# First mixture's combining and the attention behind it, as two stages and as one by groups of four tiles

## The reference, cut to what matters

```python
# mixture (the end of it): top 2 of 8 experts, dense path abel_out
gate = sigmoid(concat([abel_out, moe_out]) @ gc_w + gc_b)
mixed = abel_out * (1.0 - gate) + moe_out * gate
x = x + (residual + mixed)
# causal attention, one head of 256 channels
Q = x @ Wq.T + bq ; K = x @ Wk.T + bk ; V = x @ Wv.T + bv
scores = where(causal, einsum('btc,bsc->bts', Q, K) * scale, -inf)
w = softmax(scores)
out = einsum('bts,bsc->btc', w, V) @ Wo.T + bo
```

## Time and profile before

| | |
|---|---|
| median of 3 runs | 1505.36 us (1504.7 to 1508.71) |
| the profiled execution, its own time | 1508.83 us |
| its span in the profile | 1507.2 us |
| PE matmuls busy | 1173.9 us (78%) |
| PE weight loads busy | 1014.6 us (67%) |
| DVE busy | 805.3 us (53%) |
| ACT busy | 574.3 us (38%) |
| POOL busy | 412.2 us (27%) |

### The profile page before, as it was taken

How to read it: one execution, slowest core, us unless ns; L and a number is a source line. 1 busy time by engine, 2 the same in 40 slices (tenths; PEclk the granted TensorE clock), 3 DMA queues, 4 the chain that set the end, 5 groups by cost and what they waited for, 6 DMA issues and landing times. The chain is left out here.

```text
span 1507.2 us, 25573 instructions
## 1 busy us (share of the span) xinstructions
PE 1173.9 (78%) x7238; PEld 1014.6 (67%) x7239; DVE 805.3 (53%) x2591; ACT 574.3 (38%) x1143; POOL 412.2 (27%) x478
## 2 busy tenths in 40 slices
PE   5896887853899999910899968998863599999940
PEld 5764665742688888810779857897752488888830
DVE  6445755746345445458544464444855344544538
ACT  1112552321454555544333323332432255455545
POOL 3002101656344444400000010000576244443410
PEclk9898995866899999965899988999776799999975
DMA  9300341436543333352000000000256573333346
GB/s 294 114 0 1 146 148 57 158 137 220 198 150 107 98 100 103 95 200 68 0 1 1 1 1 1 1 1 1 113 199 220 174 247 100 101 125 98 105 166 224
DMA packets 75431, 161.10 MB, mean 107 GB/s; under 512 B 11270, under 2 KB 36562, under 8 KB 75354
## 3 DMA queue, kind: packets, MB, share of 16 engines
q1 hardware_dynamic: 54794, 104.93, 20.2%
q0 software_dynamic: 19776, 54.45, 11.5%
q10 hardware_dynamic: 784, 0.79, 0.2%
HBM read 88.66 MB, written 71.47 MB: 106 GB/s over the span
## 5 line engine op out<-in xcount | busy, mean ns | idle before, releaser
L1426 PE MATMUL bank<-ew,rows 128*128 x852 | 308.4, 362 | 4.1 <-DVE rows L1076 2.8
L1427 PE MATMUL bank<-low_in,rows 128*128 x852 | 272.7, 320 | 0.0
L1428 PE MATMUL bank<-ew,rows 128*128 x852 | 272.7, 320 | 0.0
L1217 POOL DMA_INDIRECT results<-xh x142 | 141.9, 1000 | 310.6 <-DVE xh L1096 296.0
L1426 PEld LDWEIGHTS bank<-ew,rows 128*128 128x128 f32 x852 | 163.0, 191 | 16.4 <-issue 8.9
L1428 PEld LDWEIGHTS bank<-ew,rows 128*128 128x128 f32 x852 | 161.3, 189 | 11.9
L1427 PEld LDWEIGHTS bank<-low_in,rows 128*128 128x128 f32 x852 | 162.5, 191 | 6.9
L600 POOL TENSOR_TENSOR work<-work,mhalf 128x8 f32<-128x8 f32 (+1 forms) x20 | 37.9, 1897 | 460.7 <-DVE work L593 460.0
L1105 DVE TENSOR_TENSOR rows<-bank,rows 128x512 fp32r<-128x512 f32 x142 | 98.3, 692 | 98.4 <-ACT rows L164 98.4
L1076 DVE SCALAR_TENSOR_TENSOR rows<-bank,rows 128x256 fp32r<-128x256 f32 x142 | 60.3, 425 | 164.9 <-ACT rows L169 139.0
L1198 POOL DMA_INDIRECT slots_in<-xh,work x128 | 125.9, 984 | 67.7 <-issue 35.6
(11 more groups left out here) (295 smaller groups left out, 2002.1 us busy)
## 6 DMA issues: line engine op xcount, KB each, us to landing
xh<-slots_in POOLq DMA_DIRECT2D x142, 129.0 KB
xh<-results SPq DMA_DIRECT2D x16, 1032.0 KB, 6.2
low_in<-low SPq DMA_DIRECT2D x32, 512.0 KB
residual<-xs SPq DMA_DIRECT2D x16, 512.0 KB
dense<-ab SPq DMA_DIRECT2D x16, 512.0 KB
xs<-residual SPq DMA_DIRECT2D x16, 512.0 KB
ab<-dense SPq DMA_DIRECT2D x16, 512.0 KB
xs<-in_L_attn_a_x_dram SPq DMA_DIRECT2D x4, 1024.0 KB
```

The lines of the kernel that those rows point to most:

```text
L1217: pool.indirect_dma_start(out=yg, out_offset=bass.IndirectOffsetOnAxis(ap=back[j % RING], axis=0), in_=yr[j % RING], in_offset=None).then_ ...
L1426: pe.matmul(o, hi, f32r(high(c)), start=(c == 0), stop=False)
L1427: pe.matmul(o, hi, f32r(low(c)), start=False, stop=False)
L1428: last = pe.matmul(o, lo, f32r(high(c)), start=False, stop=(stop and c == chunks[-1]))
```

## The change

`mixture(0)` now ends when its results lie in memory; combining, for the first mixture alone, is part of `attention`. There, 32 rows n run in one sequence over both batches, and between them:

- SyncE fetches results and dense part of every group, three groups ahead at first; the fetching back of the dense part during the first mixture's experts is gone (`RETURNED`).
- VectorE combines group g + 2 during the rows of group g: `gate_in` after the first row's work, `gate_out` and half of `gather` after the second, the other half after the third, statistics after the fourth. `gather` is three multiply-adds per tile straight onto `xs`; ScalarE no longer scales anything for it. Groups 0 and 1 are combined before the first row.
- The keys, queries and values of group g + 1 are prepared within the rows of group g, in half parts (one bank each, banks 7 and 3): keys in the second row, values in the third, queries in the fourth. For the group that opens the second batch (SWITCH, 4) the keys are turned in row 15, and queries and values made at row 16, since bank 3 is in use by the scores before.
- Only one group of queries is kept. The outputs of two successive rows share bank 6, so that bank 7 is free. The split parts of `wa` and `wvo` have their own places and are made once, not once per batch. `prob` moves from `work` to the place of `xh`; there is one `ln` buffer, not two.

Its core (waits of the new helper functions as they stand; those like ones shown are left out):

```diff
-                    for g in range(NG + 2):
+                    for g in range(NG + 2) if r == 1 else ():
...
-                        for o, i in ((xs, xs_out), (ab, ab_out)):
+                        for o, i in RETURNED:
...
+                    for g in range(NG):
+                        k = place(g)
+                        if g >= 3:
+                            sp.wait_ge(x2_ok, 3 * GT * (1 if g == 3 else g))
+                        sp.dma_start(y_at[k].rearrange("p t k c -> p t (k c)"), y[:, tiles(g), :]).then_inc(y_ld[k], 16)
+                        sp.dma_start(ab_at[k].rearrange("p t c -> p (t c)"), ab_out[g]).then_inc(y_ld[k], 16)
...
+                    def gate_in(g):
+
+                        y = y_at[place(g)]
+                        v.wait_ge(y_ld[place(g)], 32 * (uses(g) + 1 if place(g) == 0 else 1))
+                        small(v.tensor_tensor(zz, y[:, :, :, C], wts[:, tiles(g), :], ALU.mult))
+                        settled()
+                        small(v.tensor_reduce(z, zz, AX.X, ALU.add))
+                        settled()
+                        small(v.scalar_tensor_tensor(z, z, gcb[:], zab[:, tiles(g)], ALU.add, ALU.add))
+                        settled()
+                        v.tensor_scalar(z, z, -87.0, None, ALU.max).then_inc(z_ok, 1)
...
+                    def gather(g, half):
+
+                        y, a = y_at[place(g)], ab_at[place(g)]
+                        some = range(half * GT // 2, (half + 1) * GT // 2)
+                        done = 3 * (GT * g + half * GT // 2)
+                        for k in range(3):
+                            for m, t in enumerate(some):
+                                if k >= 1:
+                                    v.wait_ge(x2_ok, done + (k - 1) * len(some) + m + 1)
+                                o = xs[:, g * GT + t, :]
+                                src, part = ((a[:, t, :], shut[:, t:t + 1]), (y[:, t, 0, 0:C], gw2[:, t, 0:1]),
+                                             (y[:, t, 1, 0:C], gw2[:, t, 1:2]))[k]
+                                v.scalar_tensor_tensor(o, src, part, o, ALU.mult, ALU.add).then_inc(x2_ok, 1)
...
+                    def key_part(g, c):
+                        pe.wait_ge(ln_ok, GT * (g + 1))
+                        after(pe, q_ok, KC * g)
+                        after(pe, v_ok, 2 * g)
+                        if g == SWITCH:
+                            pe.wait_ge(klow_ok, KC * g + c)
+                        for t in range(GT):
+                            last = pe.transpose(bank[:, key_bank(g, c), t * P:(t + 1) * P], ln[:, t, c * P:(c + 1) * P], ident[:])
+                        last.then_inc(lnT_ps, 1)
...
+                    def query_part(g, j):
+                        pe.wait_ge(klow_ok, KC * (g + 1))
+                        pe.wait_ge(wlow_ok, 2)
+                        if g == SWITCH:
+                            pe.wait_ge(exp_ok, BT * g // GB)
+                        elif g >= 1:
+                            pe.wait_ge(v_ok, 2 * (g + 1))
+                        for c in range(KC):
+                            last = split(bank[:, query_bank(g, j), :], lambda x: weight(WA, x, c, slice(j * P, (j + 1) * P)),
+                                         lambda y: keys[:, g % GB, y, c, :], c == 0, c == KC - 1)
+                        last.then_inc(q_ps, 1)
...
+                    def value_part(g, h):
+                        pe.wait_ge(klow_ok, KC * (g + 1))
+                        pe.wait_ge(wlow_ok, 2)
+                        if g == SWITCH or g == 0:
+                            pe.wait_ge(q_ok, KC * (g + 1))
+                        for t in range(h * GT // 2, (h + 1) * GT // 2):
+                            o = bank[:, value_bank(g, h), (t % 2) * C:(t % 2 + 1) * C]
+                            for c in range(KC):
+                                split(o, lambda x: keys[:, g % GB, x, c, t * P:(t + 1) * P],
+                                      lambda y: weight(WVO, y, c, slice(0, C)), c == 0, False)
+                            last = pe.matmul(o, onesb[0:2 * QROW + 1, :], vbp[:], start=False, stop=True, skip_group_check=True)
+                        last.then_inc(v_ps, 1)
+
...
+                    gather(1, 0)
+                    gather(1, 1)
+                    statistics(1)
+                    for n in range(NR + 1):
+                        g, q = ahead(n)
+                        if n >= 1:
+                            low_shares(n - 1, slice(0, 2))
...
+                            if g and q == 1:
+                                low_keys(g, 0)
+                            if g and q == 2:
+                                low_values(g, 0)
+                            highest(n)
+                            if g and q == 1:
+                                low_keys(g, 1)
+                            if g and q == 2:
+                                low_values(g, 1)
+                            if g and q == 3:
+                                for j in range(KC):
+                                    low_queries(g, j)
...
+                                low_shares(n - 1, slice(2, None))
+                                finish(n - 1)
...
+                        now = n // GT
+                        if n < NR and n % GT == 0 and now + 1 < NG:
+                            normalise(now + 1)
+                        if n < NR and now + 2 < NG:
+                            if n % GT == 0:
+                                gate_in(now + 2)
+                            if n % GT == 1:
+                                gate_out(now + 2)
+                                gather(now + 2, 0)
+                            if n % GT == 2:
+                                gather(now + 2, 1)
+                            if n % GT == 3:
+                                statistics(now + 2)
...
+                        if n >= 1:
+                            pe.wait_ge(exp_ok, n)
+                            for c in range(min(2, (n - 1) % BT // GT + 1)):
+                                turn(n - 1, c)
+                        if switching(n):
+                            for j in range(KC):
+                                query_part(SWITCH, j)
+                            weigh_row(n - 1)
+                            scores(n)
+                            for h in range(2):
+                                value_part(SWITCH, h)
```

431 lines of the change are left out of this document (269 added, 162 removed).

## The result

The changed kernel took **1456.14 us** (median of 4 runs, 1455.16 to 1460.08), the kernel before on the same chip 1505.03 (4 runs, 1501.61 to 1508.71). The ratio is 0.9676, with a 95% interval of 0.9659 to 0.9693: 48.9 us less, where the text said 39.7 less and 1466. The profiled execution took 1455.16, near its median, while that of before took 1508.83 and lay 3.8 above its own. So the two profiles differ by 53.7 us, 4.8 more than the medians.

The account below looks back on a forecast made before the run. TensorE bounds the rows and VectorE combining, with about 97 us of TensorE idle to win. 699 + 106.9 + 30.5 + 20 + 123.2 + 32.5 = 1012.1 for 1051.8, 39.7 us less: 1466, range 1448 to 1492.

Parts of the forecast that it names:

- The start: From fetching the results to the first row maximum: it comes at 699 us instead of 754.4.
- The lengths of the groups: Times between maxima: rows 0-3 25.2 us, 4-7 32.1, 8-11 43.6, row 15 to 16 20.
- The reason for rows 0 to 3 and 16 to 19: VectorE, with 20.3 us of work for 13.6 before in rows 0 to 3, sets the pace: +12 there.
- it all hides: Rival: added work hides, rows 0 to 3 take TensorE's 16.6 us, rows 4 to 7 30; 1441 to 1450, chance 0.06.
- VectorE over 80% busy: Sign in the new profile: VectorE over 80% busy from the first maximum at 699 to the fifth at about 724.
- Combining at the price of rows: Between rows: combining and preparation together give VectorE 14.7 us per group, lengthening rows 0 to 3 by 12.
- TensorE's added work in full: Groups 1 to 3 and 5 to 7: 7.2 us each of added TensorE work, charged at its whole duration.
- The normalising: Rows 8 to 11: 1.5 us for transposes that wait for the normalising, within 43.6 for 34.6.
- VectorE's order at 1 to 2 us more per row: Rival: VectorE's strict order costs sixteen rows with both works 16 to 32 us more; 1482 to 1498, chance 0.14.
- Low clock between rows: Rival: pauses in rows 0 to 7 and 16 to 23 keep TensorE at 1.2 GHz, 72 us more; 1538, chance 0.10.
- First fetches sharing the DMA engines: Rival: before the first row, first fetches share engines instead of coming in turn, 7 us later; 1473, no separate chance.
- Behind attention: The second mixture, 455 us of the same instructions, was left unchanged in the sum.

Follow-up runs that it names:

- e5: Changed kernel with all eight groups combined before the first row and only preparation left between rows: 1465.77 us, ratio to before 0.9953.
- e6: Changed kernel with two of three multiply-adds per tile cut to 8 of 256 columns in groups 2 to 7: 1424.60 us, ratio to before 0.9672.
- e9: Changed kernel with the values' 28 matmuls issued twice for groups 1 to 3 and 5 to 7: 1443.37 us, ratio to before 0.9805.
- e2: Changed kernel with the next group's normalising moved up behind the maximum of the group's first row: 1416.48 us, ratio to before 0.9621.
- e1: The changed kernel run again without edits, as yardstick on the experiments' chip: 1423.93 us against 1472.58 before, ratio 0.9669.
- e4: Changed kernel with ScalarE's exponential ahead of second-half key and value copies and queries' copies in short rows: 1426.95 us, ratio to before 0.9689.
- e3: Changed kernel with group 1's combining moved into VectorE's waits for group 0's queries and values: 1416.84 us, ratio to before 0.9617.
- e10: Changed kernel with the edits of e2 and e3 plus statistics of group 1 and later groups made earlier: 1411.43 us, ratio to before 0.9584.
- e11: Changed kernel with the edits of e2 and e3 plus 24 unread filler matmuls in the first rows: 1408.56 us, ratio to before 0.9564.
- e12: Changed kernel with the edits of e2 and e3, early statistics and filler matmuls all together: 1410.28 us, ratio to before 0.9582.

## Why the prediction was right or wrong, point by point

**The start** was right. First maximum at 699, measured 696.86, of which 2.1 us are the experts' earlier end. Every part came within about 2 us of its forecast: gate to transposes, queries, values (at the high clock, 684.80 on, where I took a middle one), the twelve sums in 4.83 for 4.9. From ask to use the fetches took 7.2 us, where the sum had 5.4 and 1.3 for the dense part, so 0.5 more, and the ask came 1.7 earlier than the sum's 655.5. That they come in turn and not shared held: a first group's wait of 7 us more did not occur.

**The lengths of the groups** were right to 1.1 us, except for rows 16 to 19 (28.5 forecast, 25.4 measured): 25.2, 32.1, 43.6, 36.2 and 20 against 24.1, 31.1, 42.9, 35.2 and 19.2. With the start these errors make up the 11.7 us by which attention ended ahead of 1012.1. The largest is that of rows 16 to 19: the values of group 4 behind row 16 and the warm start together were charged 3.3 us over rows 0 to 3, and 1.3 was measured. All errors have the same sign; what made the small ones was not tried.

**The reason for rows 0 to 3 and 16 to 19 was wrong.** The step "VectorE has 5.6 + 14.7 = 20.3 us for 13.6 before, so it sets the pace", with some 4 us of idle time (24.0) and 1.2 of clock, gave 25.2. By the same step rows without combining take 17 to 19, as the expectation of e5 says, and e5 measured 24.14. What is there instead is TensorE: the 16.6 us at the high clock that the prediction itself names under the rival "it all hides", 2.3 more for the low clock (18.86 busy), and 5.2 of waits, for transposes' input and for exponentials. Three of the 5.2 us lie in one chain, in the timeline of the changed kernel:

```profile
698.70 0.16 DVE L1666 SCALAR_TENSOR_TENSOR work<-work 128x4 f32<-128x4 f32 x1 [1.56 <-POOL work L606]
698.90 1.38 DVE L1670 TENSOR_SCALAR work<-xs,work 128x256 f32<-128x256 f32 x4
...
700.33 1.12 PE L1879 MATMUL bank<-ident,work 128*128 128x128 f32 x4 [2.17 <-DVE work L1670]
```

The root on GpSimd (1.6 us), then the normalising, then the transposes, with TensorE idle from the maximum to 700.33 but for one transpose. That the length came out right was luck: the sum by VectorE and the sum by TensorE happened to come out alike, and a forecast that hits a length says nothing of its cause. The prediction named "VectorE over 80% busy" as what would be seen; it was at 78%, close to that, and in e5 at 55% for the same length. A busy share was no test of this step, only a change of the load is.

**Combining at the price of rows** was the second consequence of that step. The 11.6 and 15 us for rows 0 to 3 and 16 to 19 were booked to both works together; the runs give all of it to the preparation and its waits, none to combining (e5, e6).

**TensorE's added work in full** was right. The prediction charged all 7.2 us per group although weight loads fill only 26.5 of 31.1 and 37.7 of 42.9 us. e9 is the test: 28 more matmuls lengthen each group by 3.2 to 3.4 us, as much as they are busy. The Trainium skill (Perfetto Trace Analysis, Identifying the Most-Contended Engine) judges TensorE's headroom by the share of peak arithmetic and by the busy share of weight loads. By the second of these there was room for these matmuls in the groups of 31 and 43 us; here the trace disagrees, since none was absorbed with weight loads at 85 to 88%. Busy matmuls were the measure of what one more would cost.

**The normalising** in rows 8 to 11 ("1.5 for transposes that wait") was right: 1.1 measured, and e2 takes it back.

**The rivals.** VectorE's order at 1 to 2 us more per row: no, and e6 shows that its load is not what counts. All hidden, 1441 to 1450: the measured 1456 lies nearer to it than its chance of 0.06 suggests, since combining does hide in full; what kept the time above is TensorE's waits and clock, not the amount of VectorE's work. Low clock between rows, 1538: no. The granted clock stays at 1.00 from 704 on with TensorE waiting once or twice per row. The section on depth-cycling that the prediction cited from the Trainium skill (TensorE: Matmul & The Clock Gate) has such short idling swing the clock; from the rise in the first rows to row 15 it did in no profile here, and behind row 16 it fell in five profiles (e1, e4, e5, e6, e9) and did not in two with the same order there (the changed kernel's first, e3), for 1.3 us. First fetches sharing the DMA engines: no.

**Behind attention** I left everything out; it was 2.3 us, in code that is the same. For it and the 2.1 ahead no mechanism was tried, and the profiled executions lie as far from their medians (3.8 above and 1.0 below).

## What to carry to other kernels

When two engines are busy for the same share of a stretch, the profile doesn't say which one sets it: take the load off one and add to the other, one run each, and the question is answered. Here load on the engine that wasn't the bound was free, but its place was not: 2.3 us of instructions ahead of the one that the bound engine waited for cost 1.9. So move what the bound engine waits for up (e2, e3), and nothing in front of it (e4, e10). And where stages with different limits follow one another, price each moved work on its own, for here most of the gain came from the work that cost 42 us alone and nothing beside rows.

## What the runs showed of the hardware

- The same sequence of instructions behind the same waits (1.74 us busy of 4) ran at a granted clock of 1.00 in two profiles (the first, e3) and at 0.74 to 0.83 over 8 us in four others (e1, e5, e6, e9). What decided it was not found; it costs 1.3 us.
- Matmuls whose result nobody reads, put into an idle stretch of TensorE, kept the clock at 1.00 and made the real ones behind them shorter (e11: six in 0.96 us for 1.63). Where the real ones were ready earlier, the same fillers held them up by 1.9 us, and nothing was gained (e12).
- The kernel before took 1505 us where the first result was taken and 1472.3 to 1472.6 on the three chips of the experiments, 2.2% less, while rows 4 to 7 and 8 to 11 take the same to 0.05 us in both profiles. The difference lies in other stages and was not pursued.
